# A gated recurrent layer on one core: fp32 matmuls with the state h standing in four column tiles, in place of three bf16 parts

## What is computed

```python
# x (8, 512, 512): batch B=8, T=512 steps, D=512; h0 (8, 512)
def step(h, x_t):
    fused = sigmoid(concatenate([x_t, h], -1) @ w_W + w_b)     # (8, 1024)
    r, z = split(fused, 2, -1)                                 # reset, update
    memory = x_t @ wx_W + wx_b + r * (h @ wh_W + wh_b)
    h_new = z * h + (1 - z) * tanh(memory)
    return h_new, h_new
out = x + scan(step, h0, x)
```

## Time and profile before

| | |
|---|---|
| median of 3 runs | 2035.18 us |
| the profiled execution, its own time | 2036.86 us |
| its span | 2032.7 us |
| PE matmul busy | 1838.1 us (90%), 52224 matmuls |
| PE weight load busy | 1646.3 us (81%) |
| DVE busy | 1395.7 us (69%), 7191 instructions |
| ACT busy | 1076.7 us (53%) |
| POOL busy | 271.1 us (13%) |

### The profile page before, as it was taken

How to read it: one execution, slowest core, us unless ns; L and a number is a source line. 1 busy time by engine, 2 the same in 40 slices (tenths; PEclk the granted TensorE clock), 3 DMA queues, 4 the chain that set the end, 5 groups by cost and what they waited for, 6 DMA issues and landing times.

```text
span 2032.7 us, 127549 instructions
## 1 busy us (share of the span) xinstructions
PE 1838.1 (90%) x52224; PEld 1646.3 (81%) x52224; DVE 1395.7 (69%) x7191; ACT 1076.7 (53%) x5003; POOL 271.1 (13%) x1284
## 2 busy tenths in 40 slices
PE   5999999999999999999999999999999999999986
PEld 4888888888888888888888888888888888888875
DVE  6666666666666666666666666666666666666666
ACT  4555555555555555555555555555555555555544
POOL 0111111111111111111111111111111111111111
PEclk9999999999999999999999999999999999999989
DMA  5210000000000000000000000000000000000000
GB/s 177 81 45 9 9 9 8 4 8 9 9 9 3 9 8 9 9 8 4 9 8 9 9 5 7 9 8 9 9 3 9 8 9 9 8 4 9 8 9 9
DMA packets 35801, 30.00 MB, mean 15 GB/s; under 512 B 1584, under 2 KB 34352, under 8 KB 35376
## 3 DMA queue, kind: packets, MB, share of 16 engines
q1 hardware_dynamic: 35376, 23.10, 3.5%
HBM read 14.70 MB, written 8.39 MB: 11 GB/s over the span
## 4 chain that ended last, share of the span: by engine, by line
PE 71%; DVE 21%; issue 5%; DMA 1%; SPq 0%; POOL 0%; ACT 0%; POOLq 0%; DVEq 0%
PE ps L218 39%; PE ps L232 33%; DVE m_pre L377 5%; DVE h L397 5%; DVE h L392 5%; DVE h L386 4%; DVE pre_z L373 1%; DMA x_sb<-in_x 1%; PE ps L207 0%; SPq L183 0%; SPq L175 0%; DVE ps L365 0%; SPq L178 0%; POOL y L485 0%; DVE m_add L412 0%
## 5 line engine op out<-in xcount | busy, mean ns | idle before, releaser
L218 PE MATMUL ps<-wh,h 128*24 128x256 bf16 x24576 | 782.6, 276 | 166.3 <-DVE h L397 157.4
L218 PEld LDWEIGHTS ps<-wh,h 128*24 128x24 bf16 x24576 | 648.6, 123 | 261.7 <-DVE h L397 256.5
L232 PEld LDWEIGHTS ps<-h_moving,wh 128*128 128x128 bf16 x24576 | 649.3, 96 | 96.0 <-issue 96.0
L232 PE MATMUL ps<-h_moving,wh 128*128 128x24 bf16 x24576 | 698.9, 173 | 0.0
L365 DVE STREAM_TRANSPOSE ps<-ps 128x128 f32<-128x128 f32 x1024 | 271.2, 310 | 529.2 <-PE ps L218 529.2
L207 PE MATMUL ps<-x_sb,wx 128*128 (+1 forms) x3072 | 460.0, 289 | 22.4 <-DMA wx<-in_w_x 20.3
L306 ACT ACTIVATE m_by<-pre_r 128x32 f32<-128x32 f32 x512 | 133.9, 261 | 631.8 <-DVE pre_r L410 631.8
L301 ACT ACTIVATE h_moving<-h 128x48 bf16<-128x48 bf16 x1024 | 303.9, 297 | 246.3 <-DVE h L397 241.5
L472 POOL COPY m_add<-xg 128x16 f32 (+1 forms) x1024 | 186.6, 218 | 1724.1 <-DVE m_pre L377 1687.3
L207 PEld LDWEIGHTS ps<-x_sb,wx 128*128 128x128 f32 x3072 | 380.9, 192 | 22.8 <-issue 20.3
L290 ACT ACTIVATE h_by<-pre_z 128x16 f32<-128x16 f32 x1024 | 236.7, 231 | 52.4 <-DVE pre_z L373 1.2
(11 more groups left out here) (19 smaller groups left out, 122.3 us busy)
## 6 DMA issues: line engine op xcount, KB each, us to landing
x_sb<-in_x SPq DMA_DIRECT2D x32, 256.0 KB, 3.1
out_h<-y SPq DMA_DIRECT2D x32, 256.0 KB, 2.6
wh_rest<-in_w_h SPq DMA_DIRECT2D x4, 768.0 KB, 11.4
wx<-in_w_x SPq DMA_DIRECT2D x4, 768.0 KB, 11.8
h<-in_h SPq DMA_DIRECT2D x1, 16.0 KB, 1.8
bias_x<-in_b_x SPq DMA_DIRECT2D x1, 6.0 KB, 1.9
bias_h<-in_b_h SPq DMA_DIRECT2D x1, 2.0 KB, 1.7
```

Of the source, the lines that this page charges most:

```text
L218: mm = pe.matmul(ps[Q * j:Q * j + PARTS * B, RM_BANK, 0:RM], parts_of(s - 1 if s else S, k), wh[:, part, k, j * RM:(j + 1) * RM], start=(k ...
L232: mm = pe.matmul(ps[:, Z_BANK + o, ci * SLOTS * B:(ci * SLOTS + PARTS) * B], wh[:, part, k, col:col + P], h_moving[:, k // HC, k % HC, :], ...
```

## The change

h and its weights stay fp32 and there are no parts. All three gates with h now go the way of R and M before: the 8 columns of h stand, in four column tiles, and the weights move. The columns come in three groups, each with its own PSUM bank: `RM_A`, 128 columns with R and M of the first half of the outputs; `RMZ_B`, 192 columns with all three gates of the second half; `Z_A`, 64 columns with Z of the first half. For each chunk k and tile j there is one matmul a group, 48 a step.

```diff
-    PARTS = 3
+    COLS = GATES * P
+    RM_A = (0, P, 0)
+    RMZ_B = (P, P + P // 2, 1)
+    Z_A = (2 * P + P // 2, P // 2, 2)
-        wh = sb("wh", [P, PARTS, KC, N], BF16)
+        wh = sb("wh", [P, KC, TILES, COLS])
...
+            def products(group, half, s):
+                at, cols, bank = group
+                for k in range(half * HC, (half + 1) * HC):
+                    for j in range(TILES):
+                        mm = pe.matmul(ps[Q * j:Q * j + B, bank, 0:cols], h_of(s - 1 if s else S, k),
+                                       wh[:, k, j, at:at + cols], start=(k == 0), stop=(k == KC - 1),
+                                       tile_position=(0, Q * j))
...
                 pe.wait_ge(h_ready[0], nxt)
-                rm_products(range(HC), s)
+                products(RM_A, 0, s)
+                products(RMZ_B, 0, s)
                 pe.wait_ge(h_ready[1], nxt)
-                rm_products(range(HC, KC), s).then_inc(rm_done, 1)
-                pe.wait_ge(h_moved, nxt)
-                pe.wait_ge(xz_placed, nxt)
-                for o in range(HALVES):
-                    z_products(o).then_inc(z_done[o], 1)
+                products(RM_A, 1, s).then_inc(rm_a_done, 1)
+                products(Z_A, 0, s)
+                products(Z_A, 1, s).then_inc(z_a_done, 1)
+                products(RMZ_B, 1, s).then_inc(rmz_b_done, 1)
...
+            def turn(bank, o, g0, g1):
+                cols = (g1 - g0) * HC * Q
+                return dve.transpose(turned[:, o, g0:g1].rearrange("p g c q -> p (g c) q"),
+                                     ps[:, bank, 0:cols].rearrange("p (c q) -> p c q", q=Q))
...
+                dve.wait_ge(rm_a_done, nxt)
+                turn(0, 0, R, Z).then_inc(rm_a_turned, 1)
+                dve.wait_ge(rm_a_turned, nxt)
+                dve.wait_ge(x_placed, nxt)
+                sum_r(0, par, nxt)
+                dve.wait_ge(z_a_done, nxt)
+                turn(2, 0, Z, GATES).then_inc(z_a_turned, 1)
+                mix_m(0, par, nxt)
+                dve.wait_ge(z_a_turned, nxt)
+                sum_z(0, par, nxt)
+                dve.wait_ge(rmz_b_done, nxt)
+                turn(1, 1, R, GATES).then_inc(rmz_b_turned, 1)
+                dve.wait_ge(rmz_b_turned, nxt)
+                sum_r(1, par, nxt)
+                mix_h(0, s, nxt)
+                sum_z(1, par, nxt)
+                mix_m(1, par, nxt)
+                mix_h(1, s, nxt)
...
+            def hidden(o, par, nxt):
+                pool.wait_ge(rmz_b_turned if o else rm_a_turned, nxt)
+                pool.tensor_tensor(add[:, par, o, M, :, 0].rearrange("p (c b) -> p c b", b=B), product_of(o, M),
+                                   bias_h[:, HC * o:HC * (o + 1)].unsqueeze(2).to_broadcast([P, HC, B]), ALU.add)\
+                    .then_inc(hm_ready[o], 1)
```

More of the change, by code:

```diff
@@ L85, in build @@
[L85 to L98, removed]
@@ L100, in parts_of @@
-        def parts_of(s, k):
-            o, ci = divmod(k, HC)
[L103 to L114, removed]
@@ L119, in build, with product_of, x_of @@
+        def product_of(o, g):
+            return turned[:, o, g, :, 0:B]
+        def x_of(par, o, g):
+            return add[:, par, o, g, :, 1].rearrange("p (c b) -> p c b", b=B)
         bias_loaded = sem("bias_loaded")
         h0_loaded = sem("h0_loaded")
-        wh_loaded = [sem(f"wh_loaded{k}") for k in range(KC)]
-        wx_loaded = sem("wx_loaded")
+        wh_loaded = sem("wh_loaded")
+        wx_loaded = [sem(f"wx_loaded{i}") for i in range(WX_PARTS)]
+        x0_loaded = sem("x0_loaded")
@@ L411, in step @@
[L411 to L420 removed]
+                par = s % 2
@@ L488, in step @@
-            def step(t0, s, this, other, unit0, last):
-                nxt = held(pool, t0 + (s + 1))
-                if s == S and not last:
-                    pool.wait_ge(xg_ready, unit0 + UNITS)
-                if s < S or not last:
-                    pool.wait_ge(m_pre_ready[0], nxt)
-                    pool.wait_ge(m_pre_ready[1], nxt)
-                    place_xm(this if s < S else other, (s + 1) % STEPS)
-                if s % Y_HALF == Y_HALF - 1:
-                    if s == Y_HALF - 1:
-                        pool.wait_ge(y_stored, held(pool, t0 + 16))
-                    pool.wait_ge(x_loaded, 16)
-                    pool.wait_ge(h_written[0], nxt)
-                    pool.wait_ge(h_written[1], nxt)
-                    add_x(s + 1 - Y_HALF, t0 * B, y_early if s < Y_HALF else y_late)
@@ new lines, in add_x @@
+            def add_x(s, t0, nxt, after):
+                if s == 0:
+                    pool.wait_ge(y_stored, held(pool, t0 + 16))
+                pool.wait_ge(h_ready[0], after)
+                pool.wait_ge(h_ready[1], after)
+                at = s * B
+                cols = slice(t0 * B + at, t0 * B + at + B) if isinstance(t0, int) else bass.ds(t0 * B + at, B)
+                hs = h[:, s, :, 1:1 + REGION].rearrange("p o (c b w) -> p o c b w", b=B, w=TRI)[:, :, :, :, 1]
+                pool.tensor_tensor(y[:, :, s, :].rearrange("p (o c) b -> p o c b", c=HC),
+                                   x_sb[:, :, cols].rearrange("p (o c) b -> p o c b", c=HC), hs, ALU.add)\
+                    .then_inc(y_added, 1)
@@ L508, in _, with step @@
+            def step(t0, s):
+                nxt = held(pool, t0 + (s + 1))
+                for o in range(HALVES):
+                    hidden(o, s % 2, nxt)
+                add_x(s, t0, nxt, held(pool, t0 + (s + 2)))
+            pool.sem_inc(y_added, STEPS)
+            pool.wait_ge(bias_loaded, 2 * 16)
+            pool.wait_ge(x0_loaded, 16)
             with nc.Fori(0, BLOCKS - 1, engines=(mybir.EngineType.Pool,), hint_back_edge=True) as i:
                 t0 = pool.snap(i * STEPS)
-                this = bass.ds(pool.snap(i % 2), 1)
```

343 lines of the change are left out of this document (105 added, 238 removed).

## The result

| | median | range | runs |
|---|---|---|---|
| before | 2035.26 us | 2035.16 to 2042.8 | 4 |
| the change | 1989.89 us | 1988.05 to 1997.84 | 4 |

The ratio is 0.9779 (95% interval 0.9762 to 0.9796): 2.2% faster, where the prediction had 5% and 1930 us. The profiled execution took 1997.84 us, with a span of 1996.0.

The account below looks back on a forecast made before the run. It took a step as 2.8 us of products needing h plus 1.07 of small operations. Forecast: start 23.3, loop 1897 (511 steps of 3.68, 93 x 0.12, 5 more), end 8.2: span 1928, median 1930 us; own range 1860 to 1990, overall 1850 to 2110.

Parts of the forecast that it names:

- the first step starts: Start of the run: cutting of weights goes, so PE's first step waits only for 6400 KB of loads, until 23.3 us.
- 93 steps with eight products: Steps with eight input product instructions hold PE to 3.80, 0.12 us late each, in 93 steps.
- end: Behind the last step's start: h at 4.5, POOL's add 0.5, the store 3.2; 8.2 us in all.
- Removed and worth nothing more: `h_moved`, the placing of x terms in PSUM, and one POOL add a step for eight a block: no further gain.
- `mix_h` "lasts 0.24": Tail of a step on DVE: the scan starts 0.12 behind `sum_r`, lasts 0.24, and PE restarts at 3.68.
- the cost of moving columns: PE: four tiles move columns at once; rounds of 128, 192 and 64 fp32 columns take 0.109, 0.163 and 0.056 us.
- the 0.39 for an operation that the trace did not have: DVE's last transpose, of 192 columns, in a step's tail: estimated from 128-column transposes at 0.39 us.
- the 5 us by which the loop is longer than its steps: Loop before averages 3.887 us a step where the timeline's step has 3.88; so 5 us added, 1892 to 1897.
- The tiles block one another: Rival, 17%: PE starts matmuls strictly in order, only two tiles overlap, products take 5.24 us a step; 3350 us.
- The standing loads show: Rival, 10%: new fp32 weight loads on PE's tiles are exposed in 24 rounds a step; 2055 us at 10 ns each.
- One pass: Rival, 3%: an fp32 instruction moves N columns in N, PE's work falls to 1.3, steps about 3.23; 1690 us.
- is hidden by 0.21: Half 1 of h reaches PE 0.88 us after its next start, while half 0 keeps PE busy for 1.09.

Follow-up runs that it names:

- kernel 1: The change with only SP's program edited: from the ninth load of x on, loads and stores alternate, instead of stores behind all 30 loads; 1950.17 us, ratio 0.958.
- kernel 2: The change with two y buffers in turn and SP's order of loads and stores as it was; 1950.4 us, ratio 0.9579.
- kernel 3: As kernel 1, but with 23 loads ahead of the first store; 1967.79 us, ratio 0.9663.
- kernel 4: The change with POOL's adds of x to h put back to twice a block, steps 7 and 15, SP untouched; 1972.8 us, ratio 0.9684.
- kernel 5: The kernel before, with x added to h in every step and POOL's wait for the last store ahead of the first add; 2054.93 us, ratio 1.0076.
- kernel 10: Kernel 1 with POOL's `hidden` of half 1 waiting for the scan that writes h of half 0; 1982.04 us, ratio 0.9734.
- kernel 9: Kernel 1 with three input products behind each of the 16 steps, in place of four behind some; 1940.78 us, ratio 0.9532.
- kernel 7: Kernel 1 with all matmuls of a tile in a row (four instructions) in each half group before the next tile's; 1973.29 us, ratio 0.9681.
- kernel 6: Kernel 1 with `mix_h` of half 0 ahead of `sum_r` of half 1 on DVE; 1965.35 us over 7 runs, ratio 0.9651.
- kernel 8: Kernel 6 with the input products spread evenly, three in each of the 16 steps; 1961.6 us, ratio 0.9624.

## Why the prediction was right and wrong

Set against the profiled execution, the span of 1928 misses 1996.0 by 68 us, and the terms add up:

| term | forecast | measured | difference |
|---|---|---|---|
| the first step starts | 23.3 | 22.46 | -0.8 |
| loop, to the last step's start at 1987.94 | 1897 | 1965.5 | +68.5 |
| of that, the stall with the step behind it (86.14 to 136.48 to 142.02: 50.34 + 5.54 - 2 x 3.72) | 0 | 48.4 | +48.4 |
| of that, 511 steps | 3.68 | 3.72 | +20.4 |
| of that, 93 steps with eight products | 11 | 10 | -1 |
| of that, the rest | 5 | 6 | +1 |
| end | 8.2 | 8.1 | -0.1 |

The time beside the span was 1.8 us, not 4.2, and the median lies 8 us under the profiled execution, not 1.7. That 1989.89 is just inside the forecast's own range of 1860 to 1990 is luck: none of the terms that made the range holds a stall.

- **What failed** is the line "Removed and worth nothing more", in its part "one add a step on POOL in place of eight a block (POOL is busy 13% of the span)". The price was read from POOL's busy share, as if the edit only added work. Its first instruction carries the wait for `y_stored`, which moves from step 7 to step 0 of the block, and `hidden`, which is new on the chain, stands behind it. What the wait waits for was never looked up: SP's queue, where the store is behind all loads. Kernels 1, 2, 3 and 4 each take the stall away or set its size, and kernel 5 makes it in the kernel before.
- The prediction came near it. Its last sentence names an `add_x` that makes `hidden` late as something that would add to the tail, but gives it no price and doesn't look for what could make it late.
- **Mis-sized** is `mix_h` "lasts 0.24": 0.28, and with it the step of 3.68. Measured from PE's start at 1002.21, the transpose starts at 2.87 (forecast 2.84), lasts 0.38 (0.39), `sum_r` is at 3.29 (3.27) and `mix_h` at 3.38 (3.39); the whole 0.04 is the scan. POOL's `hidden`, put down as hidden behind the sigmoid, runs beside it. The scan costs 0.03 us more for it by kernel 10, 15 us over 511 steps; the rest of the 0.04 stays unexplained.
- **Right**: the cost of moving columns, 0.109, 0.163 and 0.056 a round, and with it the decision to count an fp32 instruction of N columns as 2N in bf16; the 0.39 for an operation that the trace did not have; eight products at 3.80, measured 3.83, which kernel 9 turns into the 11 us that three everywhere give; the start and the end.
- Right in size and without a reason: the 5 us by which the loop is longer than its steps. In the change nearly all of it lies around the start of the last block, where PE's starts at 1926.01 and 1943.31 are three steps apart, 17.3 us in place of 11.2; the kernel before has the like there. Its cause is open. The clock row of before has its one 8 in that stretch, the 39th slice, and not in the first and the last, as the prediction reads it.
- **The tiles block one another** (17%) is refuted by the four starts 7 ns apart, and by kernel 7, which puts four instructions on one tile in a row and loses 0.05 us a step. The Trainium skill, "TensorE: Matmul & The Clock Gate", Part 3, has matmuls keep program order in start and end; the runs disagree for column tiles. In kernel 7 the order of the program has four instructions on one tile before the next tile's first, and yet 96 take 2.84 us, with four to a round.
- **The standing loads show** (10%): the rounds of 128 columns are 0.109, as before. **One pass** (3%): 273 ns and 0.109, not half.
- Half 1 "is hidden by 0.21": right in the change (the weight loads run on without a wait), and kernels 6 and 10 show that the margin is small. Both miss 1.09 by less than 0.1 and pay.
- Without the stall the mechanism gives 1950 us (4.2%, kernels 1 and 2), 20 over the forecast: the scan. With the store in its place and three products a step it gives 1940.

## What to carry to other kernels

When an edit moves an instruction, look at the waits that it carries before its duration: what each waits for, what is queued ahead of that on its own engine or queue, and who stands behind the moved instruction. A slack of 4 us that a kernel has by luck is spent by any change that makes its steps earlier or shorter, and a once-only stall is not seen in a timeline of the middle: read the longest single wait in the view of the waits, and the clock row. And before shortening one half of a double chain, write down what the other half then lacks.

## What the runs showed of the hardware that was not expected

- Column tiles overlap even where the program gives one of them four instructions in a row: 96 take 2.84 us in place of 2.81, and the four of a round start up to 47 ns apart, not some 20.
- A scan on DVE with both inputs in SBUF takes 0.28 us beside an add on POOL, and 0.25 without it. The Trainium skill, "SBUF — State Buffer", section "SBUF: two separate sides", calls the port pair that the two engines share an exclusive lock on which the loser blocks for the whole instruction. Here POOL's add starts at 1005.55, 0.04 ahead of the scan, and lasts to 1005.76; a scan that waited for all of that would end at 1006.01, and it ends at 1005.87. The trace shows a small slowdown, not a block (POOL's spans are rough). Where both start within 0.01 us of each other (kernels 6 and 8), one of the two is slowed and the other is not: the scan takes 0.26 and the add 0.28, or the scan 0.32 and the add 0.22. Even then the scan loses 0.07 us, not the 0.22 of the add.
- A stall costs more than itself: in the 46.7 us in which PE stands idle the granted clock falls to 1.2 GHz, and the first step behind it has 4.61 us of products, against 2.81.
